# Routed experts of a mixture-of-experts block written out, with three weight buffers, four gather buffers and the weighing ahead of the inner split

## Chip, core and metric

The kernel runs on one core of one Trainium2 chip. The metric is the device time of the whole program in microseconds (us), the median of three runs. The program computes one transformer block in the order feed-forward, attention, feed-forward on 4096 tokens of width 512, all in float32. TensorE multiplies float32 through pairs of terms, a rounded high part and the remainder, which the code calls hi and lo.

## What is computed

Each of the two feed-forward layers is a mixture of 32 experts of which every token takes 6, plus one shared expert that every token takes:

```python
logits = h @ gate_w.T                      # h: 4096 x 512, 32 experts
scores = jnp.sqrt(jax.nn.softplus(logits))
_, topk_idx = jax.lax.top_k(scores + bias[None, :], K)      # K = 6
...
valid = pos < CAP                          # CAP = 192 tokens per expert
xb = jnp.zeros((E, CAP + 1, Hd), x.dtype).at[eid, pos].set(h_rep)
g = jnp.einsum('ech,eih->eci', xb, w_gate) # 512 -> 256
u = jnp.einsum('ech,eih->eci', xb, w_up)
inter = jax.nn.silu(g) * u
yb = jnp.einsum('eci,ehi->ech', inter, w_down)
y = yb[eid, pos] * w_slot[:, None]
routed = y.reshape(-1, K, Hd).sum(axis=1)
si = jax.nn.silu(h @ sg.T) * (h @ su.T)
shared = jnp.clip(si, -SWIGLU_LIMIT, SWIGLU_LIMIT) @ sd.T
return routed + shared
```

The block is `x + 0.5 * ffn(layernorm(x))`, then `x + attention(layernorm(x))`, then the feed-forward again with the same weights.

## The kernel before

Nothing is scheduled by the program at run time: each engine has its own written list, and semaphores join them. A feed-forward layer (`ffn(n)`, n is 0 or 1) has two parts that follow one another behind a barrier.

`front` normalises the tokens, runs the router and the shared expert, and builds `slots`, the row numbers of the 192 tokens of each expert. The shared expert's weights are loaded raw, split into `shared_hi` and `shared_lo` once in layer 0 (L444 on ACT, L548 on DVE), and kept to the end of the program. Toward its end SP loads the raw weights of experts 0 and 1 (L335).

`routed_experts` goes through the 32 experts. An expert's weights are 128 x 3072 numbers, 1.5 MB. For expert e:

- SP loads the raw weights as one DMA into one of two buffers `raw[u]`, as soon as the whole of the expert two before it is split.
- ACT makes `w_hi` and DVE makes `w_lo` from it, in three thirds of 1024 columns (`split`): thirds 0 and 1 are gate and up, third 2 is down.
- POOL gathers two times 96 rows of tokens into `xg` (`gather`, L899, two indirect DMAs), PE turns them (`turn`, L1111), ACT and DVE write the hi and lo of the turned rows to `xt`. DVE also copies the two columns of token weights to `wcol` and the row numbers of a later gather to `gather_idx`.
- PE runs gate and up (`gate_up`); ACT unloads the low products, DVE adds the high ones, ACT applies silu, DVE multiplies (`inter`), ACT and DVE split the result (`split_inner`: `in_hi`, `in_lo`).
- PE runs `down`; ACT weighs the result into `y` (`weigh`, L979), after it has copied the row numbers to `add_idx`.
- POOL adds the two times 96 rows of `y` to the layer's output in HBM (`scatter`, L910, two accumulating indirect DMAs). A scatter waits until the one before it has landed (`added`), since both may hit the same row.

PE goes `turn(e+2)`, `gate_up(e+1)`, `down(e)`, and again. On ACT one expert's step is in this order:

```python
turn(ni, nu); split(ni, nu, 0)      # next expert
unload_gate(i, u); split(ni, nu, 1)
gate(i, u); unload_up(i, u)
split_inner(i, u)
weigh(pi, nu)                       # the expert before
split(ni, nu, 2)
```

In layer 0 the attention weights are split beside it, one chunk of 512 columns to each of ten experts (`split_chunk`). Each engine's list is written out for the first experts and is a loop with two experts per pass for the others.

Of the kernel before, what the change touches and what calls it, by code (L numbers as in the profile page):

```python
# [64 lines left out]
NO_SLOT = 4000.0  # L65
WQKV = KB * 6 * DH
# [35 lines left out]
def allocate_kept(nc, ctx):  # L102
# [14 lines left out]
    k.shared_hi = sb("shared_hi", [P, WALL], F32R)  # L117
    k.shared_lo = sb("shared_lo", [P, WALL], F32R)
# [35 lines left out]
def front(nc, a, k, n, src, acc, accs, htab, slots, staged, raw, xs, w_loaded, y_stored):  # L154

    with ExitStack() as ctx:
# [58 lines left out]
        raw_b = beside("r_raw_b", [P, SB_, E], F32, 3, 4 * SA * E)  # L215
        if n == 0:
            raw_shared = beside("raw_shared", [P, WALL], F32, 5, 0)
# [26 lines left out]
        tab_done, turned, grouped = sem("r_tab"), sem("r_turned"), sem("r_grouped")  # L244
        if n == 0:
            setup_small, setup_shared, setup_zeroed = sem("setup_small"), sem("setup_shared"), sem("setup_zeroed")
            setup_hi, setup_lo, setup_dumps = sem("setup_hi"), sem("setup_lo"), sem("setup_dumps")
# [22 lines left out]
        with nc.Block(no_gpsimd_drain=True) as block:  # L270

            @block.sync
            def _(sp):
# [35 lines left out]
                if n == 0:  # L309
                    sp.dma_start(raw_shared[:, :], a["w_shared"]).then_inc(setup_shared, 16)  # L310
# [22 lines left out]
                for u in range(2):  # L333
                    sp.wait_ge(up_ready, FB * (PLACES - 2 + u) + FB)
                    sp.dma_start(raw[u][:, :], a["w_experts"][u, :, :]).then_inc(w_loaded[u], 16)  # L335
                    spot()
# [39 lines left out]
            def _(act):  # L376
# [14 lines left out]
                def turn(g, c):  # L391
# [3 lines left out]
                    if n == 0 and g == PLACES - 1:  # L395
                        act.wait_ge(setup_lo, 2)
# [36 lines left out]
                for g in range(G):  # L433
# [43 lines left out]
            def _(dve):  # L477
# [58 lines left out]
                for g in range(G):  # L536
# [162 lines left out]
            def _(pe):  # L699
# [120 lines left out]
def routed_experts(nc, a, k, n, htab, acc, slots, raw, xs, w_loaded, y_stored):  # L820

    with ExitStack() as ctx:
# [4 lines left out]
        THIRD = WALL // 3  # L827
# [6 lines left out]
        wcol = sb("e_wcol", [HALF, 2 * E], F32)  # L834
# [11 lines left out]
        gathered = [sem(f"e_gathered{u}_") for u in range(2)]  # L846
        added, y_free, seen = sem("e_added"), sem("e_y_free"), sem("e_seen_by_gpsimd")
        hi_ready, lo_ready = sem("e_hi_ready"), sem("e_lo_ready")
        t_ready, t_hi, t_lo, col_done = sem("e_t_ready"), sem("e_t_hi"), sem("e_t_lo"), sem("e_col_done")
# [6 lines left out]
        part = lambda t, c, m: t[:, 2 * c:2 * c + 2, m, :]  # L856
        if n == 0:
# [7 lines left out]
        high, low = (lambda bank, m=m: bank[:, :].rearrange("p (b o) -> p b o", b=FB)[:, :, m * CAP:(m + 1) * CAP]  # L865
                     for m in range(2))
        turned = lambda c: ps_t[c][:, 0:TC].rearrange("p (k s) -> p k s", k=2)

        with nc.Block(no_gpsimd_drain=True) as block:

            @block.sync
            def _(sp):
                if n == 0:
                    for c, (hi, lo, from_) in enumerate(attention_chunks):
# [19 lines left out]
            def _(pool):  # L894
# [40 lines left out]
                for i in (E // 2 - 2, E // 2 - 1):  # L935
                    for u in range(2):
                        scatter(i, u)
# [833 lines left out]
```

## Time and profile before

| | |
|---|---|
| median of 3 runs | 1680.55 us (1677.33 to 1682.53) |
| profiled execution | 1681.07 us, of which its span (first to last instruction) 1679.3 us |
| mean granted TensorE clock in it | 0.963 of full speed |
| PE busy | 1487.0 us, 89% of the span |
| DVE, ACT, POOL busy | 1115.3, 1028.6, 762.5 us |
| DMA | 255.57 MB, mean 152 GB/s |

The span falls into front 0 (to some 217 us), routed experts 0 (to some 543 us), attention (to some 1149 us), front 1 (to some 1363 us) and routed experts 1 (to the end). An engine's share over the whole span is a mean over these five. A time in the timeline is from the start of the span; the number in brackets behind an instruction is how long its engine had been idle, and what ended that. Matmuls overlap on PE, so the end of one lies a little behind the start of the next. "Turn(e)" below is PE's group of 8 transposes for expert e; there is one such group per expert, which makes them good marks.

### The profile page before, as it was taken

Reading aid. Unit: us, or ns where it says so; the run is one execution under the profiler, and the core shown is the slowest. Engines: PE = TensorE matmul, PEld = TensorE weight load, DVE = VectorE, ACT = ScalarE, POOL = GpSimd, SP = SyncE. Lnnn points to the kernel's source line nnn. Section 1 sums busy time; section 2 is a strip of 40 time slices with the busy share of each in tenths; the row PEclk is TensorE's granted clock in tenths of the full one; section 3 lists DMA queues with packets and bytes.
Section 4 is the critical chain, followed back from the end, with each engine's and each line's share of the span. In section 5 each row is a group of like instructions: output and inputs, shape, how many; then the busy total and the mean of one; then the engine's idle time right before and its main releaser. Section 6 shows DMA issues by size and latency. Waiting matters only on the chain. (4 is left out here: it accounts for less than half of the span.)

```text
span 1679.3 us, 26033 instructions
## 1 busy us (share of the span) xinstructions
PE 1487.0 (89%) x8436; PEld 1235.7 (74%) x8436; DVE 1115.3 (66%) x2284; ACT 1028.6 (61%) x2108; POOL 762.5 (45%) x659
## 2 busy tenths in 40 slices
PE   5999969899995689999999999895999869999996
PEld 4877758787774578887887887774887758877874
DVE  5659847777774357666766675664649857777774
ACT  5862437777774366666666666654762527777774
POOL 0113235555653666656557555420113225566654
PEclk9999979999998789999999999997999989999998
DMA  7736358889995211111111111015555447999995
GB/s 274 248 124 199 107 188 251 256 255 265 252 266 103 66 45 39 38 51 52 45 45 45 58 39 38 26 38 208 185 175 166 129 146 241 262 268 263 257 270 105
DMA packets 94598, 255.57 MB, mean 152 GB/s; under 512 B 19152, under 2 KB 20112, under 8 KB 86192
## 3 DMA queue, kind: packets, MB, share of 16 engines
q1 hardware_dynamic: 71984, 202.58, 35.9%
q0 software_dynamic: 22528, 51.92, 14.5%
q8 instruction: 45, 0.74, 0.2%
q14 instruction: 41, 0.34, 0.1%
HBM read 185.70 MB, written 68.76 MB: 152 GB/s over the span
## 5 line engine op out<-in xcount | busy, mean ns | idle before, releaser
L1032 DVE TENSOR_TENSOR e_w_lo<-e_raw,e_w_hi 128x1024 fp32r<-128x1024 f32 x192 | 233.7, 1218 | 109.3 <-ACT e_w_hi L947 94.5
L947 ACT ACTIVATE e_w_hi<-e_raw 128x1024 fp32r<-128x1024 f32 x192 | 202.5, 1056 | 31.9 <-PEq L270 20.9
L1551 POOL TENSOR_SCALAR t_prob<-t_prob,t_inv 128x128 f32<-128x128 f32 (+7 forms) x128 | 111.2, 869 | 221.7 <-DVE t_inv L1456 221.7
L1122 PE MATMUL e_ps_gate<-e_xt,e_w_hi 128*128 128x384 f32 x512 | 163.6, 382 | 36.3 <-DVE e_w_lo L1032 36.0
L899 POOL DMA_INDIRECT e_xg<-htab,e_gather_idx x128 | 138.3, 1081 | 64.5 <-issue 39.3
L910 POOL DMA_INDIRECT x_after_ffn<-e_y,e_add_idx x64 | 103.4, 1616 | 116.9 <-DMA x_after_ffn<-e_y,e_add_idx 93.5
L910 POOL DMA_INDIRECT out<-e_y,e_add_idx x64 | 104.0, 1624 | 108.2 <-DMA out<-e_y,e_add_idx 86.0
L1122 PE MATMUL e_ps_up<-e_xt,e_w_hi 128*128 128x384 f32 x512 | 151.8, 361 | 0.0
L353 POOL TENSOR_SCALAR d_inter<-d_inter 128x512 f32<-128x512 f32 x32 | 26.0, 811 | 267.9 <-DVE d_inter L518 267.7
L1351 ACT ACTIVATE t_prob<-a_wide,t_neg_max,a_q_scale 128x128 f32<-128x128 f32 (+7 forms) x128 | 106.5, 832 | 54.1 <-DVE t_neg_max L1450 53.7
L1122 PEld LDWEIGHTS e_ps_gate<-e_xt,e_w_hi 128*128 128x128 f32 x512 | 100.3, 196 | 46.4 <-issue 25.4
L1123 PE MATMUL e_ps_gate<-e_xt,e_w_lo 128*128 128x192 f32 x512 | 132.2, 258 | 0.0
L1123 PE MATMUL e_ps_up<-e_xt,e_w_lo 128*128 128x192 f32 x512 | 129.4, 253 | 0.0
L1358 ACT ACTIVATE t_pt<-a_bank 128x512 fp32r<-128x512 f32 x144 | 84.0, 596 | 68.3 <-PE a_bank L1627 68.1
L1461 DVE TENSOR_TENSOR t_pt<-a_bank,t_pt 128x512 fp32r<-128x512 f32 x144 | 96.2, 684 | 42.5 <-ACT t_pt L1358 41.9
L87 PE MATMUL e_ps_down<-e_w_hi,e_in_hi 128*96 128x512 f32 x256 | 101.1, 395 | 2.9 <-ACT e_y L979 2.9
L1123 PEld LDWEIGHTS e_ps_gate<-e_xt,e_w_lo 128*128 128x128 f32 x512 | 101.8, 199 | 0.0
L89 PE MATMUL e_ps_down<-e_w_hi,e_in_lo 128*96 128x512 f32 x256 | 101.5, 396 | 0.0
L88 PE MATMUL e_ps_down<-e_w_lo,e_in_hi 128*96 128x512 f32 x256 | 100.2, 391 | 0.0
L1123 PEld LDWEIGHTS e_ps_up<-e_xt,e_w_lo 128*128 128x128 f32 x512 | 97.9, 191 | 0.0
L1448 DVE TENSOR_REDUCE t_top<-a_wide 128x1 f32<-128x128 f32 (+7 forms) x128 | 95.6, 747 | 2.0 <-PE a_wide L1619 1.9
L1122 PEld LDWEIGHTS e_ps_up<-e_xt,e_w_hi 128*128 128x128 f32 x512 | 96.3, 188 | 0.0
(223 smaller groups left out, 4480.9 us busy)
## 6 DMA issues: line engine op xcount, KB each, us to landing
e_raw<-in_w_experts SPq DMA_DIRECT2D x64, 1536.0 KB
htab<-d_h SPq DMA_DIRECT2D x16, 1024.0 KB, 5.3
d_x<-in_x SPq DMA_DIRECT2D x16, 512.0 KB, 6.9
d_xs<-in_x SPq DMA_DIRECT2D x32, 256.0 KB, 3.6
x_after_ffn<-d_xs SPq DMA_DIRECT2D x32, 256.0 KB, 3.2
q_x<-x_after_ffn SPq DMA_DIRECT2D x32, 256.0 KB, 3.0
t_res<-x_after_ffn SPq DMA_DIRECT2D x32, 256.0 KB, 2.6
x_after_attention<-t_res SPq DMA_DIRECT2D x32, 256.0 KB, 2.0
```

The lines of the kernel that those rows point to most:

```text
L87: pe.matmul(out, wh, mh, start=first, stop=False)
L88: pe.matmul(out, wh, ml, start=False, stop=False)
L89: return pe.matmul(out, wl, mh, start=False, stop=last)
L899: pool.indirect_dma_start(xg[u][q][:, :], None, htab, bass.IndirectOffsetOnAxis(ap=gather_idx[u][:, q:q + 1], axis=0)).then_inc(gathered[u ...
L910: pool.indirect_dma_start(acc, bass.IndirectOffsetOnAxis(ap=add_idx[u][:, q:q + 1], axis=0), y[u][q][:, :], None, compute_op=ALU.add).then ...
L947: act.activation(w_hi[u][:, cols], raw[u][:, cols], ACT.Copy).then_inc(hi_ready, 1)
L1032: dve.tensor_tensor(w_lo[u][:, cols], raw[u][:, cols], w_hi[u][:, cols].bitcast(F32), ALU.subtract).then_inc(lo_ready, 1)
L1122: pe.matmul(out, w[0][:, c, cols], xt[u][:, c, :, :], start=c == 0, stop=False)
L1123: got = pe.matmul(out[:, 0:CAP], w[1][:, c, cols], xt[u][:, c, 0, :], start=False, stop=c == KB - 1)
L1351: act.activation(prob[:, u, 0:width(i)], ps_s[i % 2][:, 0:width(i)], ACT.Exp, scale=q_scale[:, i // H % QSLOTS, i % H:i % H + 1], bias=neg ...
L1461: dve.tensor_tensor(pt[1][g % 3][:, :], bank("prob", T, c)[:, :], pt[0][g % 3][:, :].bitcast(F32), ALU.subtract).then_inc(p_lo, 1)
L1551: pool.tensor_scalar(prob[:, u, 0:width(i)], prob[:, u, 0:width(i)], inv[:, u:u + 1], 1.0, ALU.mult, ALU.mult).then_inc(p_ready, 1)
```

## The change

1. **Written out.** The loops of `routed_experts` on all five engines become plain lists over e from 0 to 31.
2. **Three raw weight buffers by thirds.** Each third has its own DMA of 512 KB and its own semaphore. The DMA of third c of expert e+3 waits until third c of expert e is split. Expert 2's weights are now loaded at the start of the routed part, without a wait.
3. **Four gather buffers, no index copies.** `gather` and `scatter` read the row numbers in `slots`, and `weigh` takes its scale from `xg`. The copies to `gather_idx`, `add_idx` and `wcol` and the semaphores for them go. Gathers 0 to 3 are issued at once; then each scatter(e) is followed by gather(e+4).
4. **Weighing first.** On ACT `weigh(e-1)` stands ahead of `split_inner(e)`.
5. **Shared weights split anew.** `shared_hi` and `shared_lo` move to the end of SBUF, where the attention weights are written during routed experts 0, and this makes room for items 2 and 3. So `front` of layer 1 also loads and splits the shared weights.

```diff
+    k.shared_hi, k.shared_lo = (nc.alloc_sbuf_tensor_at(f"shared_{part}", [P, WALL], F32R, offset=SBUF_END - (2 - i) * 4 * WALL)
+                                for i, part in enumerate(("hi", "lo")))
...
-                if n == 0:
-                    sp.dma_start(raw_shared[:, :], a["w_shared"]).then_inc(setup_shared, 16)
+                sp.dma_start(raw_shared[:, :], a["w_shared"]).then_inc(setup_shared, 16)
...
-                        if n == 0:
-                            act.wait_ge(setup_shared, 16)
-                            for part in (slice(0, WGU), slice(WGU, WALL)):
-                                act.activation(k.shared_hi[:, part], raw_shared[:, part], ACT.Copy).then_inc(setup_hi, 1)
+                        act.wait_ge(setup_shared, 16)
+                        for part in (slice(0, WGU), slice(WGU, WALL)):
+                            act.activation(k.shared_hi[:, part], raw_shared[:, part], ACT.Copy).then_inc(setup_hi, 1)
...
+        raw = raw + [sb("e_raw2_", [P, WALL], F32)]
-        gather_idx = [sb(f"e_gather_idx{u}_", [HALF, 2], U32) for u in range(2)]
-        add_idx = [sb(f"e_add_idx{u}_", [HALF, 2], U32) for u in range(2)]
-        xg = [[sb(f"e_xg{u}{q}_", [HALF, ROW], F32) for q in range(2)] for u in range(2)]
+        xg = [[sb(f"e_xg{r}{q}_", [HALF, ROW], F32) for q in range(2)] for r in range(GATHERED)]
...
+                for c in range(3):
+                    load_weights(2, c)
...
+                for e in range(E - 3):
+                    for c in range(3):
+                        sp.wait_ge(lo_ready, 3 * e + c + 1)
+                        load_weights(e + 3, c)
...
-                with pool.Fori(2, E // 2 - 1) as i:
-                    for u in range(2):
-                        gather_next(i, u)
-                        scatter(i - 1, u)
...
+                for e in range(GATHERED):
+                    gather(e)
+                for u in range(XS):
+                    pool.wait_ge(y_stored[u], 16 * ((NT - 1 - u) // XS + 1))
+                for e in range(E):
+                    scatter(e)
+                    if e + GATHERED < E:
+                        gather(e + GATHERED)
...
+                def weigh(e):
+                    if e >= 2:
+                        act.wait_ge(added, 32 * (e - 1))
+                    for q in range(2):
+                        act.wait_ge(d_ready, 2 * e + q + 1)
+                        act.activation(y[e % 2][q][:, :], ps_down[q][0:HALF, :], ACT.Copy,
+                                       scale=xg[e % GATHERED][q][:, D + e:D + e + 1]).then_inc(y_ready, 1)
...
+                    gate(e)
+                    unload_up(e)
+                    if e:
+                        weigh(e - 1)
+                    split_inner(e)
+                    if ahead:
+                        split(e + 1, 2)
...
+                turn(0)
+                for e in range(E):
+                    if e + 1 < E:
+                        turn(e + 1)
+                    gate_up(e)
+                    if e:
+                        down(e - 1)
+                down(E - 1)
```

On PE the order of turns, gates, ups and downs is what it was, except that turn(2) to turn(31) no longer stand in a loop.

**POOL at the start of the routed part.** Before, from the barrier on. One number ends the name of every buffer of a kind, so `e_xg_0` stands for all of them; x4 is gather(0) and gather(1). Then come gathers 2, 3 and 4, scatter(0), gather(5) and scatter(1):

```order
L919 COPY e_gather_idx_0<-slots 96x2 x2
L899 DMA e_xg_0<-htab,e_gather_idx_0 96x544 x4
L899 DMA e_xg_0<-htab,e_gather_idx_0 96x544 [waits e_col_done0]
L899 DMA e_xg_0<-htab,e_gather_idx_0 96x544
L899 DMA e_xg_0<-htab,e_gather_idx_0 96x544 [waits d_y_stored4_0,d_y_stored5_0,d_y_stored3_0,e_col_done0,d_y_stored2_0,d_y_stored0_0,d_y_stored1_0]
L910 DMA x_after_ffn<-e_y_0,e_add_idx_0 4192x512 [waits e_y_ready0]
L910 DMA x_after_ffn<-e_y_0,e_add_idx_0 4192x512 [waits e_y_ready0,e_added0]
```

Now, the same place. The x8 are gathers 0 to 3; then scatter(0), gather(4), scatter(1), gather(5):

```order
L899 DMA e_xg_0<-htab,slots 96x544 x8
L907 DMA x_after_ffn<-e_y_0,slots 4192x512 [waits d_y_stored4_0,d_y_stored3_0,d_y_stored5_0,d_y_stored2_0,e_y_ready0,d_y_stored1_0,d_y_stored0_0]
L907 DMA x_after_ffn<-e_y_0,slots 4192x512
L899 DMA e_xg_0<-htab,slots 96x544 x2
L907 DMA x_after_ffn<-e_y_0,slots 4192x512 [waits e_added0,e_y_ready0]
```

Before, gather(e+5) was the one behind scatter(e) from scatter(0) on; now it is gather(e+4).

**ACT, one expert's step in the middle of routed experts 0.** Before (`wo_hi` is the attention chunk):

```order
L965 ACTIVATE e_silu_0<-e_gate_sum 128x384 [waits e_gate_sum_ready0]
L961 ACTIVATE e_up_low<-e_ps_up 128x384 [waits e_up_ready0]
L970 ACTIVATE e_in_hi_0<-e_inter_0 128x384 [waits e_mul_ready0]
L976 ACTIVATE e_add_idx_0<-slots 96x2 [waits e_col_done0,e_y_free0]
L979 ACTIVATE e_y_0<-e_ps_down_0,e_wcol 96x512 [waits e_d_ready0] x2
L947 ACTIVATE e_w_hi_0<-e_raw_0_57 128x1024 [waits e_w_loaded0_0]
L1002 ACTIVATE wo_hi<-d_xs_0 128x512 [waits e_att_loaded2_0]
```

Now:

```order
L940 ACTIVATE e_silu_0<-e_gate_sum 128x384 [waits e_gate_sum_ready0]
L936 ACTIVATE e_up_low<-e_ps_up 128x384 [waits e_up_ready0]
L952 ACTIVATE e_y_0<-e_ps_down_0,e_xg_0 96x512 [waits e_d_ready0,e_added0]
L952 ACTIVATE e_y_0<-e_ps_down_0,e_xg_0 96x512 [waits e_d_ready0]
L945 ACTIVATE e_in_hi_0<-e_inter_0 128x384 [waits e_mul_ready0]
L923 ACTIVATE e_w_hi_0<-e_raw_0_59 128x1024 [waits e_w_loaded02_0]
L958 ACTIVATE wo_hi<-d_xs_0 128x512 [waits e_att_loaded1_0]
```

The two `e_y` have moved ahead of `e_in_hi`, the index copy is gone, and each third of the weights has a semaphore of its own.

## Rows read from the trace of the kernel before

**Rows 1.** Windows: length, busy time by engine, PEclk, DMA share, GB/s
```profile
251.62:508.17 256.55, 232.64 (x1458) 201.73 (x1456) 190.60 (x344) 190.24 (x343) 145.74 (x109) 1.00 0.89 257
508.17:543.40 35.23, 19.04 (x108) 15.44 (x108) 12.80 (x21) 14.78 (x29) 14.04 (x10) 0.86 0.51 89
1393.22:1643.54 250.32, 233.81 (x1457) 203.09 (x1456) 184.30 (x333) 184.92 (x332) 147.69 (x109) 0.99 0.90 259
1643.54:1679.30 35.76, 19.03 (x109) 15.40 (x107) 13.11 (x22) 14.86 (x29) 13.87 (x10) 0.87 0.51 90
```

**Rows 2.** Timeline of PE: turns of several experts, and one last down matmul
```profile
240.68 1.54 PE L1111 MATMUL e_ps_t<-ident,e_xg 96*128 96x96 f32 x8 [4.03 <-DMA e_xg<-htab,e_gather_idx]
...
1370.20 1.54 PE L1111 MATMUL e_ps_t<-ident,e_xg 96*128 96x96 f32 x8 [8.54 <-DMA e_xg<-htab,e_gather_idx]
...
1383.59 1.54 PE L1111 MATMUL e_ps_t<-ident,e_xg 96*128 96x96 f32 x8 [3.60 <-DMA e_xg<-htab,e_gather_idx]
...
1392.99 0.39 PE L89 MATMUL e_ps_down<-e_w_hi,e_in_lo 128*96 128x512 f32 x1
1393.22 0.82 PE L1111 MATMUL e_ps_t<-ident,e_xg 96*128 96x96 f32 x8
...
1401.27 0.82 PE L1111 MATMUL e_ps_t<-ident,e_xg 96*128 96x96 f32 x8
...
1580.70 0.87 PE L1111 MATMUL e_ps_t<-ident,e_xg 96*128 96x96 f32 x8 [1.69 <-DMA e_xg<-htab,e_gather_idx]
```

**Rows 3.** Waits: us in total, times, longest
```profile
POOL out L910 <- DMA out<-e_y,e_add_idx: 86.0, 29, 6.2
...
PE e_ps_t L1111 <- DMA e_xg<-htab,e_gather_idx: 36.8, 14, 12.1
PE e_ps_gate L1122 <- DVE e_w_lo L1032: 36.0, 48, 1.6
```

**Rows 4.** Timeline of ACT and of DVE, around one weighing
```profile
437.12 0.53 ACT L970 ACTIVATE e_in_hi<-e_inter 128x384 fp32r<-128x384 f32 x1 [1.35 <-DVE e_inter L1058]
437.65 1.24 ACT L979 ACTIVATE e_y<-e_ps_down,e_wcol 96x512 f32<-96x512 f32 x2
...
439.87 1.22 DVE L1032 TENSOR_TENSOR e_w_lo<-e_raw,e_w_hi 128x1024 fp32r<-128x1024 f32 x1 [1.63 <-ACT e_w_hi L947]
441.94 0.20 DVE L1042 TENSOR_SCALAR e_wcol<-e_xg  x2
```

**Rows 5.** Timeline of POOL: an early gather, and first halves of scatters 0, 19, 20
```profile
1367.02 0.94 POOL L899 DMA_INDIRECT e_xg<-htab,e_gather_idx  x1 [0.31 <-issue]
...
1395.09 1.51 POOL L910 DMA_INDIRECT out<-e_y,e_add_idx  x1 [5.21 <-ACT e_y L979]
...
1569.55 1.51 POOL L910 DMA_INDIRECT out<-e_y,e_add_idx  x1 [2.84 <-DMA out<-e_y,e_add_idx]
...
1579.79 1.47 POOL L910 DMA_INDIRECT out<-e_y,e_add_idx  x1 [4.12 <-DMA out<-e_y,e_add_idx]
```

**Rows 6.** The page's groups of POOL's indirect DMAs: busy, mean ns of one
```profile
L899 POOL DMA_INDIRECT e_xg<-htab,e_gather_idx x128 | 138.3, 1081 | 64.5 <-issue 39.3
...
L910 POOL DMA_INDIRECT out<-e_y,e_add_idx x64 | 104.0, 1624 | 108.2 <-DMA out<-e_y,e_add_idx 86.0
```

**Rows 7.** Timeline of POOL: first halves of the last two scatters, without weight loads
```profile
1666.29 1.41 POOL L910 DMA_INDIRECT out<-e_y,e_add_idx  x1 [3.66 <-ACT e_y L979]
...
1673.01 1.41 POOL L910 DMA_INDIRECT out<-e_y,e_add_idx  x1 [3.59 <-issue]
```

**Rows 8.** Timeline of DVE and PE where the shared expert starts, in both fronts
```profile
22.16 3.43 DVE L548 TENSOR_TENSOR shared_lo<-raw_shared,shared_hi 128x2048 fp32r<-128x2048 f32 x2 [1.11 <-ACT shared_hi L444]
...
1165.56 0.69 DVE L502 TENSOR_TENSOR ht_lo<-d_ps_t,ht_hi 128x512 fp32r<-128x512 f32 x1 [0.23 <-ACT ht_hi L399]
...
1169.84 0.63 PE L87 MATMUL d_ps_gate<-ht_hi,shared_hi 128*128 128x512 f32 x1
```

More of the change, by code:

```diff
@@ L65 @@
 NO_SLOT = 4000.0
+THIRD = WALL // 3
+GATHERED = 4
 WQKV = KB * 6 * DH
@@ L856, in routed_experts @@
         part = lambda t, c, m: t[:, 2 * c:2 * c + 2, m, :]
+        third = lambda t, c: t[:, c * THIRD:(c + 1) * THIRD]
+        high, low = (lambda bank, m=m: bank[:, :].rearrange("p (b o) -> p b o", b=FB)[:, :, m * CAP:(m + 1) * CAP]
+                     for m in range(2))
+        turned = lambda c: ps_t[c][:, 0:TC].rearrange("p (k s) -> p k s", k=2)
+        attention_chunks = []
         if n == 0:
@@ L887, in _, with load_weights @@
-                with sp.Fori(E // 4, E // 2 - 1) as i:
-                    for u in range(2):
-                        e = 2 * i + u
-                        sp.wait_ge(lo_ready, 3 * e + 3)
-                        sp.dma_start(raw[u][:, :], a["w_experts"][bass.ds(e + 2, 1), :, :].rearrange("o p c -> p (o c)")).then_inc(w_loaded[u], 16)
+                def load_weights(e, c):
+                    sp.dma_start(third(raw[e % 3], c), third(a["w_experts"][e, :, :], c)).then_inc(w_loaded[e % 3][c], 16)
@@ L925, in _ @@
+                        pool.indirect_dma_start(acc, row, y[e % 2][q][:, :], None, compute_op=ALU.add).then_inc(added, 16)
+                for e in range(GATHERED):
+                    gather(e)
                 for u in range(XS):
                     pool.wait_ge(y_stored[u], 16 * ((NT - 1 - u) // XS + 1))
-                gather_next(1, 0)
-                scatter(0, 0, first=True)
-                gather_next(1, 1)
-                scatter(0, 1)
-                with pool.Fori(2, E // 2 - 1) as i:
-                    for u in range(2):
-                        gather_next(i, u)
-                        scatter(i - 1, u)
@@ L941, in _, with split @@
             def _(act):
-                act.sem_inc(y_ready, 2)
-                def split(i, u, c):
-                    cols = slice(c * THIRD, (c + 1) * THIRD)
-                    act.wait_ge(w_loaded[u], 16 * i + 16)
-                    act.activation(w_hi[u][:, cols], raw[u][:, cols], ACT.Copy).then_inc(hi_ready, 1)
-                def turn(i, u):
-                    e = 2 * i + u
+                def split(e, c):
+                    act.wait_ge(w_loaded[e % 3][c], 16 * (e // 3) + 16)
+                    act.activation(third(w_hi[e % 2], c), third(raw[e % 3], c), ACT.Copy).then_inc(hi_ready, 1)
@@ L1002, in split_chunk @@
                     act.activation(hi, xs[c % XS][:, :], ACT.Copy).then_inc(att_hi, 1)
-                split(0, 0, 0)
-                split(0, 0, 1)
-                turn(0, 0)
-                split(0, 0, 2)
-                step(0, 0, behind=False)
-                pairs = len(attention_chunks) // 2 if n == 0 else 0
-                for i in range(pairs):
-                    step(i, 1)
-                    split_chunk(2 * i)
-                    step(i + 1, 0)
-                    split_chunk(2 * i + 1)
@@ L1083, in split_chunk, with turn @@
                     dve.tensor_tensor(lo, xs[c % XS][:, :], hi.bitcast(F32), ALU.subtract).then_inc(att_split, 1)
[L1085 to L1099 removed]
+                split(0, 0)
+                split(0, 1)
+                turn(0)
+                split(0, 2)
+                for e in range(E):
+                    ahead = e + 1 < E
+                    if ahead:
+                        turn(e + 1)
+                        split(e + 1, 0)
+                    add_gate(e)
+                    if ahead:
+                        split(e + 1, 1)
+                    add_up(e)
+                    gate(e)
+                    split_inner(e)
+                    if ahead:
+                        split(e + 1, 2)
+                    if 0 <= e - 1 < len(attention_chunks):
+                        split_chunk(e - 1)
             @block.tensor
             def _(pe):
[L1103 to L1105 removed]
+                def turn(e):
+                    pe.wait_ge(gathered[e % GATHERED], 32 * (e // GATHERED) + 32)
                     for c in range(2):
[L1107 removed]
+                        if e:
+                            pe.wait_ge(t_lo, 2 * (e - 1) + c + 1)
                         for b in range(2):
```

275 lines of the change are left out of this document (91 added, 184 removed).

## The prediction

> **What bounds the kernel now.** I read the windows first, to cut the routed experts into start, steady part and tail; then the timeline of PE at the turns, and the list of waits; then the timeline of POOL, ACT and DVE around one expert. In each the question is which wait ends last. The fronts and the attention are touched in one place only (below).
>
> The steady part, turn(3) to turn(31), is 28 experts: 256.55 us in layer 0 (9.16 an expert) and 250.32 us in layer 1 (8.94), together 506.87 [rows 1]. PE alone needs less: between turn(3) and turn(4) nothing held it, and they are 1401.27 - 1393.22 = 8.05 us apart [rows 2]. The difference goes to two waits, for DVE's second third of `w_lo` (36.0 us, 48 times) and for a gather (36.8 us, 14 times) [rows 3].
>
> Behind the first wait is a loop of ACT and DVE: `in_hi`, `y` (1.24 us), `w_hi`, then DVE's `w_lo`, which sat idle for 1.63 us, and so on to the next `in_hi` [rows 4]. ACT is idle for 1.35 us just before `in_hi`, and the weighing stands behind it.
>
> Behind the second is POOL. Scatter(e) starts only when scatter(e-1) has landed: 29 of 32 scatters of layer 1 waited for that, and 86.0 us in all [rows 3]. So POOL is as busy as the others, though its busy time is 147.69 of 250.32 us [rows 1]. And the gather behind each scatter lands later still: scatter(19) began at 1569.55, and PE got gather(24), issued behind it, at 1580.70, 11.15 us later, having waited for it [rows 5, 2].
>
> Three rings are thus close together: ACT and DVE at about 8.9, POOL at about 8.9, PE at 8.05.
>
> **The change, part by part.**
>
> *Weighing first, no copies.* ACT weighs in the 1.35 us in which it waited, so the ring loses 1.24 us for `y`, and `wcol` (0.20) and the two index copies (some 0.25) with it [rows 4]: 8.9 - 1.7 = 7.2 us, in layer 0 with an attention chunk 7.8. That is below PE's 8.05. This ring is out, and the 36.0 us would come back if nothing else held PE.
>
> *Weights by thirds, three buffers.* A third is asked for two experts ahead, against one, so weights are not late. The bytes are the same. The 64 more DMAs of each layer are issued on SP, which nothing waits for here.
>
> *Gathers.* This is the part that I hold to decide. Before, gather(e+5) followed scatter(e); now gather(e+4) does. PE's list is turn(e+3), gate_up(e+2), down(e+1), turn(e+4) after down(e). So the way from the end of down(e) over y(e), scatter(e) and gather(e+4) to turn(e+4) has one expert's time of PE, where it had two. Call it X. From turn(e+2) to the end of down(e) PE takes 8.05 + 0.16 = 8.21 us (1392.99 + 0.39 ends 0.16 behind the turn at 1393.22 [rows 2]). Then down(e) to turn(e+4) is X. That closes a ring over two experts:
>
> time of an expert = (8.21 + X) / 2, if this is over 8.05.
>
> X has two pieces. From the end of down to the start of the scatter, with POOL free: 1395.09 - 1393.38 = 1.71 us [rows 5, 2]; some 0.8 of this is the second half of the weighing, the rest POOL's start. From the scatter's start to the turn, G, two bounds:
> - below, with nothing else in flight: two scatter issues at a mean of 1.62, two gather issues at 1.08 [rows 6], three gaps of 0.30, and 2.24 us from the end of an issue to the turn (1367.02 + 0.94 to 1370.20 [rows 5, 2]): G = 8.54. With the shortest issues (1.41 [rows 7] and 0.94) it is 7.84.
> - above, as now: a scatter lands 8.94 - 0.85 = 8.1 us after its start when each start waits for the landing before, and gather(24) was taken 1.76 us after scatter(19) had landed (1579.79 - 0.85 = 1578.94, 1580.70 [rows 5, 2]). This is 9.85 at a place where PE waited; I take 9.7 as typical.
>
> How much of the difference stays is unknown, since no row has loads of 512 KB beside gathers. The same bytes go, but a request is a third as long. I take G = 9.0, nearer to the lower end. X = 10.71, an expert takes (8.21 + 10.71) / 2 = 9.46 us, and 56 of them 529.8: **+22.9 us**.
>
> For this step the Trainium skill has a rule ("DMA: Bandwidth & Descriptors", Queues, rings and completion order): a DMA engine goes round its queues and drains a whole packet of one before it turns to the next. By it a gather would stand behind a third of what it stood behind, G would by estimate be 8.54 and a third of 1.16, some 8.9, and the sum 1680; no row here shows packets' order.
>
> *Start.* Four gathers are out at once, so turn(2) no longer waits its 4.03 and 3.60 us [rows 2], and gate_up(1) behind it does not run at the lower clock, as turn(2) does at 1.54 us against 0.82. Turn(3) would come 8.05 after 240.68 - 4.03 and after 1383.59 - 3.60, at 244.7 and 1388.0, against 251.62 and 1393.22: 6.9 + 5.2. The copies saved (0.6 each) and expert 2's weights, which now fly beside the first gathers, I put together at 0.4 against it: **-11.7 us**.
>
> *Tail.* Now 35.76 us from turn(31) to the end [rows 1], since scatter(31) waits for a backlog. With y prompt: PE ends down(30) at 8.05 + 7.4 + 0.16 = 15.6, scatter(30) starts at 17.3, scatter(31) one unloaded step later (1673.01 - 1666.29 = 6.72 [rows 7]) at 24.0, the end 6.3 after this at 30.3. That is 5.4 less, and about 5.0 in layer 0: **-10.4 us**.
>
> *Shared weights split anew.* In layer 0 DVE's split began 1.11 us after its last turn and took 3.43 [rows 8]. In layer 1 that turn ended at 1166.25, so the split would end at 1170.8, and the first gate matmul, at 1169.84 [rows 8], starts 1.0 later: **+1.0 us**. Nothing, if ACT and DVE catch up behind (both have idle time there), up to 4.5 if all of it stays, with the 1.5 MB ahead of the constants.
>
> *Sum.* +22.9 - 11.7 - 10.4 + 1.0 = +1.8 on the profiled execution's 1681.07 us (span 1679.3, within 0.6 of the median): **1683 us**. In terms of G: 1431 + 28 G.
>
> **Rivals.**
>
> *The ring stays loaded (slower).* Gathers and scatters meet the same traffic, G = 9.7: an expert takes 9.8, the sum 1702. It decides from G = 9.1 on. For it: weights, gathers and scatters already fill 0.90 of the DMA engines [rows 1], with the same bytes now. Against: an expert is longer, so traffic is thinner. The skill ("GPSIMD Engine Reference", Specifications) adds a reason: GpSimd contends with VectorE instructions that have two SBUF inputs, as `w_lo` has. The trace agrees as far as it goes: a scatter issue takes 1.41 us when DVE is at rest [rows 7] and 1.62 in the mean [rows 6]; if the new order sets two more issues on a `w_lo`, G gains about 1 us and the sum 28.
>
> *The ring runs free (faster).* Small requests leave gathers as good as alone, G = 7.9 to 8.5: an expert takes 8.9 to 9.2, the sum 1652 to 1669. For it: the last scatters step at 6.72 us, 2.2 under the loaded step. Against: that was without any weights in flight.
>
> *Gathers are not late after all (much faster).* Were X under 8, PE would run at 8.05 to 8.3 and the time be 1604 to 1618. The issues alone take 6.3 of it with 1.71 ahead, so I see no way, unless I misread the lists.
>
> *The front costs more.* 3.5 us more at worst, inside the range.
>
> **How the numbers follow.** About 0.3%, 5 us, is what a measurement can tell from no change. Forecast, G 8.6 to 9.4, 1672 to 1694: 0.45. Loaded, above 1694: 0.25. Free, 1652 to 1671: 0.20. PE-bound, under 1620: 0.10. Faster is free, PE-bound and the forecast's lowest sixth (G under 8.7), 0.38; slower is loaded and the forecast's part with G over 9.15, 0.38; the rest, 0.24, is no change. The range 1652 to 1704 leaves out the PE-bound case and the end of the loaded one.
>
> **What would show it.** PE's wait for `e_w_lo` all but gone; its wait for `e_xg` up from 36.8 us to some 56 x 1.4 = 79 us, and the longest item; every second turn waiting for more than 2 us or each for 1.4; scatters waiting for `y` on ACT, not for the landing; turn(31) to the end at 30 us; turn(3) at 245 in layer 0. Wrong, if turns come every 8.1 us without a wait for `e_xg`, if scatters still wait for landings 29 times a layer, or if ACT's `e_y` waits for `added`.

## The result and the profile after

The changed kernel takes 1855.58 us (median of 4 runs, 1846.81 to 1856.55), the kernel before 1681.54 in the same comparison: ratio 1.103, 95% interval 1.101 to 1.105, slower. The forecast was 1683 us. The profiled execution's span is 1853.3 us, 174.0 more than before.

Windows of the changed kernel, as in [rows 1]: turn(3) to turn(31) and turn(31) to the end, of both layers:

```profile
247.60:596.20 348.60, 256.96 (x1458) 228.50 (x1456) 196.37 (x265) 196.59 (x322) 158.25 (x112) 0.84 0.73 191
596.20:625.20 29.00, 18.49 (x108) 15.39 (x108) 10.40 (x15) 12.81 (x22) 12.35 (x8) 0.91 0.43 55
1472.90:1823.80 350.90, 260.92 (x1458) 232.75 (x1457) 190.45 (x255) 190.48 (x310) 157.00 (x112) 0.84 0.72 186
1823.80:1853.30 29.50, 20.00 (x109) 16.27 (x107) 10.40 (x15) 13.25 (x22) 12.38 (x8) 0.86 0.44 54
```

The steady part holds it all: 699.5 us against 506.87, that is 192.6 more, 12.49 us an expert. In layer 0 PE is busy for 257 of 349 us, its mean clock has gone from 1.00 to 0.84, and the same bytes flow at 191 GB/s where they flowed at 257.

Waits of the changed kernel, as in [rows 3]:

```profile
PE e_ps_t L1050 <- DMA e_xg<-htab,slots: 208.4, 33, 11.7
POOL out L907 <- ACT e_y L952: 167.8, 18, 21.0
POOL x_after_ffn L907 <- ACT e_y L952: 160.2, 17, 20.8
```

PE waits for gathers, 208.4 us where it was 36.8; its wait for `e_w_lo` has left the list; POOL waits for `y` at every second scatter, and for landings 14 times a layer (65 us in all) where it was 29 times. These are in the main the signs that the forecast named. The size is another. One pair of experts in layer 1 shows it, first on PE (turn(16), the last down matmul of expert 14, turns 17 and 18; two gate matmuls for their length):

```profile
1639.03 1.54 PE L1050 MATMUL e_ps_t<-ident,e_xg 96*128 96x96 f32 x8 [6.41 <-DMA e_xg<-htab,slots]
...
1640.91 0.57 PE L1061 MATMUL e_ps_gate<-e_xt,e_w_hi 128*128 128x384 f32 x1
...
1649.08 0.39 PE L91 MATMUL e_ps_down<-e_w_hi,e_in_lo 128*96 128x512 f32 x1
1649.31 0.82 PE L1050 MATMUL e_ps_t<-ident,e_xg 96*128 96x96 f32 x8
...
1650.26 0.36 PE L1061 MATMUL e_ps_gate<-e_xt,e_w_hi 128*128 128x384 f32 x1
...
1664.51 1.54 PE L1050 MATMUL e_ps_t<-ident,e_xg 96*128 96x96 f32 x8 [7.05 <-DMA e_xg<-htab,slots]
```

then on POOL, scatter(14) and gather(18), and on SP's queue the loads of thirds:

```profile
1650.47 1.47 POOL L907 DMA_INDIRECT out<-e_y,slots  x1 [8.91 <-ACT e_y L952]
1652.24 1.89 POOL L907 DMA_INDIRECT out<-e_y,slots  x1 [0.30 <-issue]
1654.44 1.27 POOL L899 DMA_INDIRECT e_xg<-htab,slots  x1 [0.30 <-issue]
1656.01 1.29 POOL L899 DMA_INDIRECT e_xg<-htab,slots  x1 [0.30 <-issue]
...
1652.84 8.32 SPq L876 DMA_DIRECT2D e_raw<-in_w_experts  x4
```

and in windows: PE's busy stretch, its wait, and the stretch behind the wait:

```profile
1649.30:1657.30 8.00, 8.00 (x53) 7.00 (x51) 6.18 (x9) 6.55 (x11) 5.92 (x4) 1.00 0.68 143
1657.30:1664.50 7.20, 0.16 (x1) 0.00 (x0) 2.08 (x3) 2.04 (x3) 4.27 (x4) 0.75 1.03 298
1664.50:1675.60 11.10, 11.09 (x52) 10.27 (x53) 5.24 (x7) 4.96 (x8) 1.59 (x2) 0.70 0.57 148
```

In the forecast's terms: W, from turn(16) to the end of down(14), is 1649.47 - 1639.03 = 10.44 us (forecast 8.21). X is 1664.51 - 1649.47 = 15.04 (10.71), and G in it 1664.51 - 1650.47 = 14.04 (9.0): the four issues end at 1657.30, 6.83 us after the scatter's start, and the gather is then in flight for **7.21 us**, not 2.24. Two experts take 25.5 us. The pair shown is among the long ones. In the mean over the even turns 6 to 28 of both layers (24 pairs) W is 10.61, the scatter starts 1.01 after down, the four issues take 6.92 and the flight is 6.77 (5.89 to 7.41), so that G is 13.69. Only the even turn waits; when PE gets to the odd one its rows are there. DMA engines are full (1.03, 298 GB/s) just while the even gather flies: four thirds of weights go out with it. And behind 7 us without work PE runs at the lower of its two clock levels at first: the same gate matmul takes 0.57 us, later 0.36.

### The profile page after: what moved, and what is told of

Read it like the earlier page. It is cut to its first block and busy times, and to the rows that moved or that the text cites. A ratio compares the mean times of both kernels' runs of the same rounds, so it can differ in the third digit from the quotient of the medians.

```text
span 1853.3 us, 23935 instructions
## 1 busy us (share of the span) xinstructions
PE 1536.9 (83%) x8436; PEld 1291.5 (70%) x8436; DVE 1118.4 (60%) x2094; ACT 1037.5 (56%) x2046; POOL 772.7 (42%) x655
## 5 line engine op out<-in xcount | busy, mean ns | idle before, releaser
L1050 PE MATMUL e_ps_t<-ident,e_xg 96*128 96x96 f32 x512 | 74.8, 307 | 208.4 <-DMA e_xg<-htab,slots 208.4
L1050 PEld LDWEIGHTS e_ps_t<-ident,e_xg 96*128 96x128 f32 x512 | 63.9, 180 | 227.8 <-DMA e_xg<-htab,slots 223.2
L1061 PE MATMUL e_ps_gate<-e_xt,e_w_hi 128*128 128x384 f32 x512 | 202.4, 449 | 0.0
L907 POOL DMA_INDIRECT out<-e_y,slots x64 | 106.8, 1669 | 209.7 <-ACT e_y L952 167.8
L907 POOL DMA_INDIRECT x_after_ffn<-e_y,slots x64 | 103.9, 1623 | 206.1 <-ACT e_y L952 160.2
L899 POOL DMA_INDIRECT e_xg<-htab,slots x128 | 144.5, 1129 | 58.0 <-issue 38.4
L993 DVE TENSOR_TENSOR e_xt<-e_ps_t,e_xt 128x384 fp32r<-128x384 f32 x128 | 68.1, 554 | 142.2 <-ACT e_xt L928 90.6
L928 ACT ACTIVATE e_xt<-e_ps_t 128x384 fp32r<-128x384 f32 x128 | 58.5, 484 | 168.6 <-PE e_ps_t L1050 127.9
L952 ACT ACTIVATE e_y<-e_ps_down,e_xg 96x512 f32<-96x512 f32 x128 | 86.9, 682 | 71.9 <-PE e_ps_down L91 71.7
L1061 PEld LDWEIGHTS e_ps_gate<-e_xt,e_w_hi 128*128 128x128 f32 x512 | 124.8, 244 | 0.1
```

What stands on the lines that cost most here:

```text
L899: pool.indirect_dma_start(xg[e % GATHERED][q][:, :], None, htab, row).then_inc(gathered[e % GATHERED], 16)
L907: pool.indirect_dma_start(acc, row, y[e % 2][q][:, :], None, compute_op=ALU.add).then_inc(added, 16)
L952: act.activation(y[e % 2][q][:, :], ps_down[q][0:HALF, :], ACT.Copy, scale=xg[e % GATHERED][q][:, D + e:D + e + 1]).then_inc(y_ready, 1)
L1050: got = pe.transpose(ps_t[c][:, at:at + HALF], xg[e % GATHERED][q][:, (2 * c + b) * P:(2 * c + b + 1) * P], k.ident[0:HALF, 0:HALF])
L1061: pe.matmul(out, w[0][:, c, cols], xt[e % 2][:, c, :, :], start=c == 0, stop=False)
```

## The experiments

Ratios are to the kernel before in the same comparison, with 95% intervals. The kernel before had medians of 1675.02 to 1681.54 us in these comparisons. "Steady" is turn(3) to turn(31) of both layers, per expert, in the one profiled execution.

| run | us | ratio | steady |
|---|---|---|---|
| before | 1681.54 | 1 | 9.05 |
| changed | 1855.58 | 1.103 (1.101 to 1.105) | 12.49 |
| e1 five buffers | 1663.65 | 0.993 (0.991 to 0.995) | 9.04 |
| e2 gather first | 1669.57 | 0.994 (0.991 to 0.997) | 9.15 |
| e3 weights whole | 1827.09 | 1.090 (1.085 to 1.095) | 11.96 |
| e4 weigh last | 1828.5 | 1.091 (1.087 to 1.095) | 12.03 |
| e5 no loads | 1687.51 | 1.006 (1.004 to 1.009) | 9.37 |
| e6 before, swapped | 1827.98 | 1.090 (1.084 to 1.096) | 11.81 |
| e7 five, first | 1627.03 | 0.971 (0.967 to 0.975) | 8.27 |
| e8 five, whole | 1680.89 | 1.002 (0.999 to 1.004) | 9.26 |
| e9 48 transposes | 1846.5 | 1.101 (1.099 to 1.103) | 12.44 |
| e10 five, first, weigh last | 1653.46 | 0.986 (0.984 to 0.988) | 8.77 |
| e11 five, first, late load | 1617.78 | 0.965 (0.963 to 0.967) | 8.30 |
| e12 76 transposes | 1799.8 | 1.075 (1.072 to 1.078) | 11.49 |

**The place of the gather: e1, e2, e6.** Theory: the gather that stands one expert later behind the scatter makes the ring. Rivals: thirds, or the new order on ACT. e1 gives the gather its old distance with a fifth buffer:

```diff
-GATHERED = 4
+GATHERED = 5
```

> The changed kernel with five gather buffers in place of four, so that gather(e+5) follows scatter(e), as in the kernel before, and the way from down(e) to turn(e+5) has two experts' time of PE. Late gather (the ring over two experts, 12.7 us an expert in the changed kernel, is due to the gather's place): PE waits for e_xg fall from 208 us to under 30, turns come every 8.1 to 8.8 us, PE's clock stays at the upper level, time 1620 to 1660 us. Bunched weights (the loads in thirds are what holds up gathers, wherever they stand): gathers stay 6 to 7 us in flight behind their issue and PE keeps waiting for half of them, time over 1700 us.

e2 keeps four buffers and lets the gather go ahead of the scatter:

```diff
 def scatter(e):
-    pool.wait_ge(y_ready, 2 * e + 2)
...
+    pool.wait_ge(y_ready, 2 * e + 2)
+    if e + GATHERED < E:
+        gather(e + GATHERED)
     scatter(e)
-    if e + GATHERED < E:
-        gather(e + GATHERED)
```

> The changed kernel, but gather(e+4) is issued ahead of scatter(e) instead of behind it, both after y(e). Late gather: the way from down(e) to turn(e+4) loses the two scatter issues, some 3.6 us, and with shorter idle time PE's clock drops less, so two experts take 19 to 22 us in place of 25.5: time 1680 to 1760 us. Bunched weights: the gather still meets the loads, 7 us in flight, only the 3.6 us per two experts go: about 1755 us or more.

e6 does to the kernel before, with its whole loads, its two raw buffers and its old ACT order, that one thing alone, in the loop shown and in the two experts written out ahead of it:

```diff
 for u in range(2):
-    gather_next(i, u)
     scatter(i - 1, u)
+    gather_next(i, u)
```

> The kernel before, with one part of the change alone: in POOL's list each scatter(e) is followed by gather(e+4) and not by gather(e+5) (scatter and gather change places, two gather buffers, copies, whole weights and ACT's order as before). The gather's place decides by itself: a ring over two experts as in the changed kernel, and y comes still later, since ACT weighs behind in_hi: over 1800 us, PE waiting for e_xg 200 us or more. It takes the other parts too (loads of 512 KB, weighing first): under 1720 us.

e1 and e2 take away the whole loss of some 190 us, and end 0.7% and 0.6% below the kernel before. Neither is quite where I expected it: e1 lies 4 us above its range and e2 10 us below its own. In e1 PE's wait for `e_xg` is 68.6 us, 26 times, where I had put under 30, and POOL waits for landings again:

```profile
POOL x_after_ffn L907 <- DMA x_after_ffn<-e_y,slots: 80.2, 27, 5.2
POOL out L907 <- DMA out<-e_y,slots: 69.7, 24, 4.9
```

e6 makes the kernel before nearly as slow as the changed one, 9.0% against 10.3%, with 160.5 us of PE's wait for `e_xg`, less than the 200 expected. A scatter, and the turn behind it, in its layer 1; then turn(3) to turn(31):

```profile
1606.64 1.47 POOL L910 DMA_INDIRECT out<-e_y,e_add_idx  x1 [6.62 <-issue]
...
1617.52 1.54 PE L1111 MATMUL e_ps_t<-ident,e_xg 96*128 96x96 f32 x8 [4.67 <-DMA e_xg<-htab,e_gather_idx]
...
1462.80:1792.70 329.90, 263.80 (x1457) 235.17 (x1456) 195.38 (x337) 191.04 (x337) 148.46 (x112) 0.86 0.69 202
```

So the gather's place alone is enough for most of the loss, and without it none is left. G is 10.88 us here and not 14.04. In the mean over the same 24 even turns the issues take 6.05 us (6.92 in the changed kernel) and the flight 4.79 (6.77). This kernel loads whole weights, but differs in more than that; e3 below changes the loads alone.

**Is the flight long because of the loads? e5.** The loads of experts 3 to 31 are left out, so that these experts are computed with the weights of 0 to 2; the output is not the reference's, the work on every engine is the same:

```diff
 for e in range(E - 3):
-    for c in range(3):
-        sp.wait_ge(lo_ready, 3 * e + c + 1)
-        load_weights(e + 3, c)
...
-    act.wait_ge(w_loaded[e % 3][c], 16 * (e // 3) + 16)
+    act.wait_ge(w_loaded[e % 3][c], 16)
```

> The changed kernel (four gather buffers, gather(e+4) behind scatter(e)) without the weight loads of experts 3 to 31: the raw buffers keep the weights of experts 0 to 2, so the result is not the reference's, all other work stays. Weights as the reason that G, from a scatter's start to the turn that takes the gather behind it, is 14 us and not the 9.0 of the prediction: with none in flight G falls to 8.5 to 9, PE idles 2 us every second expert and keeps its upper clock, two experts take 18.5 to 19 us: 1660 to 1690 us. Gather and scatter queue on each other in POOL's own queue, whatever SP loads: the gathers of every second expert stay at 6 us or more in flight, time above 1800 us.

Timeline of POOL and PE in layer 1: one scatter's first issue, the gather's second issue, the turn:

```profile
1503.90 1.46 POOL L904 DMA_INDIRECT out<-e_y,slots  x1 [2.19 <-ACT e_y L949]
...
1509.44 1.29 POOL L896 DMA_INDIRECT e_xg<-htab,slots  x1 [0.30 <-issue]
...
1512.96 0.88 PE L1047 MATMUL e_ps_t<-ident,e_xg 96*128 96x96 f32 x8 [0.78 <-DMA e_xg<-htab,slots]
```

G is 9.06 us with issues as long as in the changed kernel (6.83 us) and a flight of 1512.96 - 1510.73 = 2.23. The scatter still stands ahead of the gather in POOL's queue, so that this is not what makes the flight long. PE does not wait 2 us at every second turn, as I expected, but mostly about 1 us at every turn (85.7 us, 56 times). An expert takes 9.37 us, where the forecast had 9.46; the profiled execution is the fastest of nine, 14.7 us under their median, and at the median it would be 9.6 at most. What the forecast described is close to the kernel without weight loads.

The changed kernel shows the same by itself. Its turn(30) comes when the last weights are in. The gather's second issue and the turn, in layer 0:

```profile
583.49 1.28 POOL L899 DMA_INDIRECT e_xg<-htab,slots  x1 [0.30 <-issue]
...
587.27 0.88 PE L1050 MATMUL e_ps_t<-ident,e_xg 96*128 96x96 f32 x8 [2.34 <-DMA e_xg<-htab,slots]
```

The flight is 587.27 - 584.77 = 2.50 us, the 24 even ones before it took 5.89 to 7.41.

**How much of the rest is the clock? e9 and e12.** Ahead of each even turn from 4 on PE gets transposes of a constant, which change no result; e9 has 48, e12 76:

```diff
 def turn(e):
+    if e >= 4 and e % 2 == 0:
+        pe.wait_ge(t_lo, 2 * (e - 1) + 1)
+        for _ in range(48):
+            pe.transpose(ps_t[0][:, 0:HALF], k.ident[0:HALF, :], k.ident[0:HALF, 0:HALF])
```

> The changed kernel, with 48 more transposes of a constant on PE ahead of each turn(e) with even e from 4 on: they fill some 4.9 us of the 7 us in which PE waits for the gather, and change no result. If the clock explains why the stretch from an even turn to the end of the next down takes 10.3 us and not 8.2 (the 8 transposes at 1.54 us against 0.82), that stretch goes back towards 8.2 and two experts take some 23.4 us against 25.4, 28 pairs of them 55 us less: about 1800 us, ratio 0.97 to the changed kernel, and 1.07 to the kernel before. If the long stretch has another cause (gate_up waiting for ACT's and DVE's parts of the turned rows, or for weights), the time stays at 1855 us, or grows by what the transposes overrun the wait.

> As the run with 48 transposes of a constant ahead of each even turn, but with 76. The 48 took 4.12 us at full clock and left PE idle for 2.8 to 3.4 us before the gather was there; the turn behind them still came out at 0.98 to 1.54 us and the first gate matmuls at 0.57 us against 0.36. 76 take some 6.5 us and leave well under 1 us. If the idle stretch itself is what costs the clock, the turn comes back to 0.82 us, the stretch from the even turn to the end of the next down to 8.2 us, two experts take 23.2 us, and the time is 1790 to 1800 us (1855 us without transposes). If the clock falls whatever PE does there, or if transposes of this kind do not hold it, the transposes themselves slow down to 0.16 us each and overrun the wait by up to 5 us in each pair, and the time is above 1860 us; should they stay fast and the gate matmuls still take 0.57 us, it stays near 1847 us.

e9 alone would have misled me: the ratio falls by 0.002 only. Its rows say why. Behind the transposes PE still stood idle for 2.07 to 4.50 us at every even turn but turn(30), and each time the gate matmuls then took 0.57 us. In e12 it is idle for 1.7 us at most, mostly under 1:

```profile
1591.34 6.43 PE L1046 MATMUL e_ps_t<-ident 96*128 96x96 f32 x76
1598.31 0.88 PE L1054 MATMUL e_ps_t<-ident,e_xg 96*128 96x96 f32 x8 [0.54 <-DMA e_xg<-htab,slots]
...
1599.31 0.36 PE L1065 MATMUL e_ps_gate<-e_xt,e_w_hi 128*128 128x384 f32 x1
```

The turn is back at 0.88, the gate matmul at 0.36, and the time at 1799.8 us, as expected: 55.8 us less than the changed kernel by the medians, 56.3 in the steady part of the profiled executions, 2.0 for each of 28 pairs (47 us by the ratios, 1.075 against 1.103). W is 8.22 us in the mean, where it was 10.61, and the flight is as before, 6.85. The clock's part is shown.

**The other parts of the change, in the slow ring: e3, e4.** e3 loads each expert's weights as one DMA of 1.5 MB, which waits until the whole of the expert three before it is split (one line of several is shown); e4 weighs behind the inner split:

```diff
-    sp.dma_start(third(raw[e % 3], c), third(a["w_experts"][e, :, :], c)).then_inc(w_loaded[e % 3][c], 16)
+    sp.dma_start(raw[e % 3][:, :], a["w_experts"][e, :, :]).then_inc(w_loaded[e % 3][0], 16)
```

> The changed kernel with each expert's weights as one DMA of 1.5 MB on one semaphore, still three buffers. Late gather: the gathers of every second expert take 3 to 4 us in flight or 7 us as now, in either case two experts take 21 to 25.5 us: 1740 to 1855 us. Bunched weights: the loads of 512 KB were what made a gather take 7.2 us in flight in place of 2.3 to 3.3, two experts take 25.5 - 4.5 and the lower clock's 2 us go too: 1680 to 1710 us.

```diff
-    if e:
-        weigh(e - 1)
     split_inner(e)
+    if e:
+        weigh(e - 1)
```

> The changed kernel with ACT's order as before: split_inner(e), then weigh(e-1). Late gather: y comes no earlier, so nothing is gained: 1850 to 1900 us. Weighing first as the cause (ACT waits for the end of down(e-1) with in_hi and the third w_hi behind it, and then the three thirds' loads go out together just as the gather flies): the loads spread, gathers fly 3 to 4 us, time 1720 to 1780 us.

By the ratios e3 is 1.2% and e4 1.1% faster than the changed kernel, and neither takes away the loss. For e4 this is outside both ranges that I expected. My reasoning, that `y` comes later and the ring gets longer, does not hold: in the even experts the scatter starts 1.01 us after down in both kernels. The means over the same 24 pairs show where the time went. In e3 the flight is 5.59 us against 6.77 and the issues are the same. In e4 the flight is 6.39, the issues 6.50 against 6.92, and W 10.29 against 10.61. When a load starts relative to the gather has moved in both; I did not isolate it, so why these terms shrink stays open.

**The same parts where the ring is gone: e7, e8, e10, e11.** e7 joins e1 and e2. e8 is e1 with whole loads. e10 is e7 with e4's order. e11 is e7 with expert 2's load held back:

```diff
+sp.wait_ge(gathered[1], 32)
 for c in range(3):
     load_weights(2, c)
```

> The changed kernel with five gather buffers and gather(e+5) issued ahead of scatter(e). In the run with five buffers PE still waited 69 us for e_xg, while 51 of 64 scatters waited for the landing before. If what is left is the gather's lateness: the waits for e_xg go, turns come every 8.3 us, 1625 to 1645 us. If it is POOL's chain of scatters (3.6 us to issue two, 4.6 to land, 0.85 to start, 9.0 an expert): the same 9.0 an expert, 1655 to 1670 us, and ACT's e_y or PE wait for it instead.

> The changed kernel with five gather buffers and each expert's weights as one DMA of 1.5 MB. Thirds help: they are asked for earlier and land sooner, so with whole loads the time is 0.5 to 1.5% over the 1664 us of the run with thirds. Thirds make no difference, since POOL's chain of scatters sets 9.0 us an expert either way: within 0.4% of it. Thirds hurt (three requests of many small rows instead of one): 0.5% or more under it, about 1650 us.

> Five gather buffers and gather(e+5) ahead of scatter(e), as in the fastest kernel so far (1627 us), but with the weighing behind the inner split, as before the change. If weighing first takes the ring of ACT and DVE below PE's 8.05 us, as the prediction had it, this ring is back at about 8.9 us here, PE waits for the second third of w_lo again, and 56 experts of 8.9 against 8.26 give +36 us: about 1662 us. If the three buffers by thirds had already taken the slack out of that ring, it stays within 5 us of 1627 us. If weighing first costs (y ready earlier is of no use, in_hi later is), it is a few us faster.

> The same kernel (five buffers, gather first, weighing first), with the load of expert 2's weights held back until gathers 0 and 1 have landed. If that load is why turn(0) comes 6 us after the issues of gather(0) now and 2.2 us in the kernel before, turn(0) comes some 3.5 us earlier in each layer and the time is 1620 us, 7 us less. If the ten gathers that go out at once delay each other, turn(0) moves by under 1 us and the time stays at 1627 us. Should expert 2's weights then be late, turn(3) comes later than 19.5 us behind turn(0).

e7, windows from turn(3) to turn(31):

```profile
244.70:478.10 233.40, 227.35 (x1458) 201.40 (x1457) 187.06 (x263) 188.23 (x318) 153.43 (x108) 1.00 1.02 281
1359.50:1589.20 229.70, 226.09 (x1458) 200.81 (x1456) 181.29 (x253) 183.53 (x309) 154.51 (x108) 1.00 1.03 281
```

PE is busy for 98% of it, 8.27 us an expert against 8.05 at best. With the old order on ACT (e10) an expert takes 8.77, 1.6% of the time by the ratios, and DVE waits for ACT inside its thirds again:

```profile
DVE e_w_lo L987 <- ACT e_w_hi L923: 99.5, 70, 2.1
```

(26.2 us in e7). So weighing first is worth 1.6% once no gather is in the way, and the ring without it takes 8.8 us, near the forecast's 8.9; in the slow ring it cost 1.1%. Whole loads cost 0.9% beside five buffers (e8 against e1), and gained 1.2% beside four.

e11 is the fastest: 1617.78 us, 3.5% under the kernel before. Gather(0)'s first issue and turn(0) in layer 1, of the changed kernel:

```profile
1444.34 1.04 POOL L899 DMA_INDIRECT e_xg<-htab,slots  x1 [9.76 <-POOLq L273]
...
1453.52 1.54 PE L1050 MATMUL e_ps_t<-ident,e_xg 96*128 96x96 f32 x8 [11.67 <-DMA e_xg<-htab,slots]
```

and of e11:

```profile
1329.25 1.05 POOL L900 DMA_INDIRECT e_xg<-htab,slots  x1 [9.75 <-POOLq L273]
...
1333.94 1.54 PE L1051 MATMUL e_ps_t<-ident,e_xg 96*128 96x96 f32 x8 [7.18 <-DMA e_xg<-htab,slots]
```

9.18 us become 4.69. In e7, which has the same gathers as e11 and the load at once, it is 8.96 (9.23 in layer 0, where e11 has 4.61): it was expert 2's load, not the gathers, that made turn(0) late.

## Why the prediction was wrong

The mechanism was the right one, a ring over two experts from down over weighing, scatter and gather to the turn, and the formula (W + X) / 2 holds: (10.44 + 15.04) / 2 = 12.7 for the pair shown, and 12.7 from the means of 24 pairs, with 12.49 over the whole steady part. Both sizes put into it were too small.

**G, in the step "Gathers", is the step that failed.** It was taken at 9.0 and bounded above by 9.7, "as now"; it measured 13.69 in the mean. Of this the issues are 6.92, where the forecast had 6.3, and the flight is 6.77, where 9.0 left 2.7.

The upper bound does not follow from the row that it was drawn from. Scatter(19) began at 1569.55 and PE took gather(24) at 1580.70, having waited for it for 1.69 us: there G is 11.15, as the forecast itself says further up. The bound used the mean step of a scatter less 0.85, that is 8.1 us, in place of the 9.39 after which this scatter landed. The gather's second issue:

```profile
1574.72 0.95 POOL L899 DMA_INDIRECT e_xg<-htab,e_gather_idx  x1 [0.30 <-issue]
```

It ends at 1575.67, and the flight is 5.03 us, not 2.24. Eight of the turns 5 to 31 of the kernel before waited for more than 0.3 us, with G from 9.49 to 11.15. With 11.15 the forecast's formula gives 1431 + 28 x 11.15 = 1743 us, already outside its range. A higher price still, of a gather taken at once beside loads, stood elsewhere in the trace. In the kernel before, SP's load of expert 2's weights, POOL's second issue of gather(2), and the window from its end to turn(2):

```profile
1374.50 10.39 SPq L882 DMA_DIRECT2D e_raw<-in_w_experts  x2
...
1375.57 0.92 POOL L899 DMA_INDIRECT e_xg<-htab,e_gather_idx  x1 [0.30 <-issue]
...
1376.50:1383.60 7.10, 3.50 (x25) 3.28 (x24) 4.23 (x7) 3.81 (x6) 1.89 (x2) 0.98 0.90 296
```

The issue ends at 1376.49, and turn(2) took the rows at 1383.59 [rows 2]: 7.10 us, beside 296 GB/s. I had used that turn only for the start, as a wait of 3.60 us to be removed. With 7.1 for the flight the upper bound would have been 6.3 + 7.1 = 13.4, near the 13.69 measured, and the rival "stays loaded" would have reached some 1431 + 28 x 13.4 = 1806 us. Without loads the flight is 2.32 in the mean of the even turns (e5), with them 6.77. The issues' part, 0.6 us of G, goes the way that the rival's second reason had it, DVE's `w_lo` beside POOL's issues; no run separates it.

**W, taken at 8.21 at the full clock, is the second.** The forecast saw the turn at 1.54 us behind a wait [rows 2] and used it for the start only. In the ring each even turn stands behind such a wait, and W is 10.61 in the mean. The Trainium skill ("TensorE: Matmul & The Clock Gate", Part 1) has PE's clock gate halve the clock when the array has been idle, and shows a loop in which the wait for a DMA between groups of matmuls brings this about each time round; the trace agrees, 0.57 against 0.36 us for the same matmul, and e12 gives 56 us of it back.

The steady part came out 699.5 - 529.8 = 169.7 us above the forecast. Without loads (e5) it is 524.7, so that the loads' part is 174.8. Of it 56.3 goes with the clock (e12: 321.17 + 322.07 = 643.2). The other 118.5 I put down to the flight: it is 4.45 us longer than in e5 in each of 24 pairs, 107 us. As e5's profiled execution is 14.7 us under its median, both figures may be that much too high. In the pair shown loads and gather start together (1652.84 and 1654.44), since the splits that free thirds run while PE and POOL finish the expert; that each pair does so is read from the trace, not tried.

**The rule on queues** did not carry what the forecast took from it. The rule of the Trainium skill ("DMA: Bandwidth & Descriptors", Queues, rings and completion order) speaks of packets. What the profile counts as packets did become a third as long. SP's queue from 1500 to 1600 us, before and in the changed kernel: packets, MB, share of the engines:

```profile
q1 hardware_dynamic: 1596, 17.45, 51.1%
...
q1 hardware_dynamic: 3456, 12.58, 41.4%
```

That is 10.9 KB in the mean before and 3.6 KB now. The gather's flight did not follow: 7.10 us beside the whole load at turn(2) before, 7.21 beside thirds, and in e3, the changed kernel with whole loads, 5.59 in the mean against 6.77 with thirds. So the step from a third of the packet to a third of the delay, and G = 8.9 by it, is not borne out; the runs do not show in what order the packets go.

**The ring of ACT and DVE** was sized well (e10), PE's floor too (e7: 8.27 in the mean).

**Start**, forecast -11.7 (-6.9 and -5.2, with 0.4 against), measured -4.0 in layer 0 (turn(3) at 247.60 against 251.62 [rows 1]) and 0.0 in layer 1: from gather(0)'s issue to turn(3) it is 1472.91 - 1444.34 = 28.57 us now, and 1393.22 - 1364.66 = 28.56 before, its gather(0) being issued at 1364.66. Turn(2) no longer waits, as forecast; but expert 2's load, put at 0.4 with the copies against it, delays turn(0) by 3.6 in layer 1 (9.18 against 5.54), the same mistake as in G on a smaller scale; with the load held back (e11) turn(0) comes 4.3 earlier than in e7.

**Tail**, forecast -10.4: 29.50 against 35.76 in layer 1, 29.00 against 35.23 in layer 0 [rows 1], -12.5. Right to 2 us.

**Shared weights split anew**, forecast +1.0 at the first gate matmul. ACT, DVE and PE in front 1 of the changed kernel:

```profile
1231.26 1.28 ACT L383 ACT_TABLE_LOAD   x1 [8.77 <-PEq L1203]
...
1249.14 3.43 DVE L551 TENSOR_TENSOR shared_lo<-raw_shared,shared_hi 128x2048 fp32r<-128x2048 f32 x2 [1.11 <-ACT shared_hi L447]
...
1252.71 0.47 PE L89 MATMUL d_ps_gate<-ht_hi,shared_hi 128*128 128x512 f32 x1 [1.10 <-DVE shared_lo L551]
```

From the table load to that matmul it is 21.45 us, against 1169.84 - 1149.53 = 20.31 before: +1.14, the wait of 1.10 that the row shows. By gather(0) it is made up for: 213.08 us from the table load, against 215.13. So it costs nothing in the end, as the forecast allowed, and the front is 2 us shorter; why it is shorter was not tried.

Together: +192.6 - 4.0 - 12.5 - 2.1 = +174.0, the difference of the spans.

## What to carry to other kernels

When a change puts a transfer on the critical path, take its price from a row in which somebody waited for that transfer from its issue on, with the same neighbours in the DMA engines, and take that row whole: a mean put in place of one of its parts turned 11.15 into 9.7 here. A transfer that was issued early shows only that it was early enough. A ring that makes PE wait for over 6 us in every second round pays twice, once for the wait and once for the slow matmuls behind it (1.54 us for a turn); waits of about 1 us in each round did not cost the clock (e5, 0.88 us for a turn). Try a change of order again when the bound has moved: weighing first and loads by thirds cost 1.1% and 1.2% in the slow ring, and gained 1.6% and 0.9% outside it.

## What the runs showed that I had not expected

A gather of 96 rows twice flies for 2.23 us with no weight loads, and for 7.21 beside four loads of 512 KB at 298 GB/s. Cutting the loads into thirds did not shorten it: with whole loads it was 5.59 in the mean, with thirds 6.77.

Behind 4.12 us of transposes at the full clock and 2.81 us of idle PE the gate matmuls ran at 0.57 us, the lower level (e9); behind 6.43 us of them and 0.54 us of idle PE they ran at 0.36 (e12). In e5 they ran at 0.36 behind a wait of 3.40 us, and fell to 0.57 after the first ones behind waits of 2.06 and 2.44, so the length of the wait just before does not settle it by itself.

The issue of a scatter takes 1.41 us with DVE at rest [rows 7] and up to 2.51 in the changed kernel (2.59 before): POOL's row, and DVE's of the same moment:

```profile
1659.62 2.51 POOL L907 DMA_INDIRECT out<-e_y,slots  x1 [2.32 <-DMA out<-e_y,slots]
...
1659.58 1.23 DVE L987 TENSOR_TENSOR e_w_lo<-e_raw,e_w_hi 128x1024 fp32r<-128x1024 f32 x1 [0.39 <-ACT e_w_hi L923]
```

This one is off the path, as the odd turns don't wait. That DVE lengthens it is what the rows suggest; no run was made to show it.
